# Scan layer: 24 of 64 diagonal blocks by ScalarE, step size times u one product earlier, TensorE's slots in another order

## The reference

```
xn = layernorm(x) * ln_w + ln_b
xin, z = split(xn @ W_in.T)                      # 256 channels each
u = silu(causal_depthwise_conv(xin, 4 taps) + conv_b)
dt, Bm, Cm = split(u @ W_xproj.T)                # 8, 16, 16
delta = softplus(dt @ W_dt.T + b_dt);  A = -exp(A_log)
for each position:                               # state h: 256 channels x 16
    h = exp(delta * A) * h + (delta * u) * Bm
    y = sum_n h * Cm
y = (y + u * D) * silu(z);  out = y @ W_out.T
```

## Time and profile before

| | |
|---|---|
| median of 3 runs | 9299.93 us (9296.48 to 9304.48) |
| the profiled execution's own time | 9299.72 us |
| its span | 9297.9 us |
| TensorE, matmuls | 8821.4 us busy, 95% |
| VectorE | 8554.3 us, 92% |
| ScalarE | 8027.6 us, 86% |
| GpSimd | 5789.4 us, 62% |
| mean granted TensorE clock | 0.989 of full speed |

### The profile page before, as it was taken

One profiled execution on the slowest core, in us unless ns is written; L12 is line 12 of the kernel. 1 busy time (PEld: TensorE's weight loads), 2 busy tenths in 40 slices (PEclk: granted clock), 3 DMA queues, 4 the chain that ended last, 5 costly groups with the idle time before them and its releaser, 6 DMA issues. The chain is left out here.

```text
span 9297.9 us, 445960 instructions
## 1 busy us (share of the span) xinstructions
PE 8821.4 (95%) x199690; PEld 3709.6 (40%) x199690; DVE 8554.3 (92%) x7167; ACT 8027.6 (86%) x12777; POOL 5789.4 (62%) x2582
## 2 busy tenths in 40 slices
PE   7999999999999999999999999799999999999999
PEld 4555555555555555555555555322222222222211
DVE  7999999999999999999999999799999999999998
ACT  6888888888888888888888888599999999999999
POOL 6999999999999999999999999500000000000000
PEclk9999999999999999999999999899999999999999
DMA  4333333333333333333333333211111111111100
GB/s 118 97 95 90 84 83 88 96 100 95 84 86 80 100 95 95 85 86 79 86 85 85 87 86 85 62 34 34 32 32 35 34 32 34 34 32 32 32 23 19
DMA packets 394196, 638.79 MB, mean 69 GB/s; under 512 B 97872, under 2 KB 98610, under 8 KB 391778
## 3 DMA queue, kind: packets, MB, share of 16 engines
q1 hardware_dynamic: 389184, 608.56, 25.0%
q10 hardware_dynamic: 2498, 1.00, 0.0%
q0 software_dynamic: 608, 0.70, 0.0%
HBM read 270.13 MB, written 71.30 MB: 37 GB/s over the span
## 5 line engine op out<-in xcount | busy, mean ns | idle before, releaser
L1094 DVE TENSOR_TENSOR_SCAN arena<-arena,carried,ps 128x512 f32<-128x512 f32 x3968 | 4757.9, 1259 | 279.1 <-PE ps L510 265.1
L942 POOL TENSOR_TENSOR arena<-arena 128x1024 f32<-128x1024 f32 x2048 | 4805.1, 2404 | 87.0 <-PE ps L521 36.5
L811 ACT ACTIVATE arena<-arena,a_neg 128x512 f32<-128x512 f32 x4096 | 2662.4, 710 | 16.8 <-DVE arena L1094 10.0
L510 PE MATMUL ps<-arena 64*32 64x128 f32 x131072 | 2310.8, 276 | 74.8 <-DVE arena L1094 41.3
L1159 DVE SCALAR_TENSOR_TENSOR arena<-arena,neg_p 128x2048 f32<-128x2048 f32 x1024 | 2350.4, 2344 | 0.1
L510 PEld LDWEIGHTS ps<-arena 64*32 64x32 f32 x131072 | 1850.6, 106 | 1197.1 <-DVE arena L1094 658.5
L880 ACT ACTIVATE arena<-ps,b2t 128x1024 f32<-128x1024 f32 (+1 forms) x2048 | 2023.0, 1052 | 203.4 <-PE ps L642 203.4
L642 PE MATMUL ps<-arena,w2s 32*32 32x512 f32 x32768 | 1514.8, 599 | 105.4 <-ACT arena L880 86.2
L886 ACT ACTIVATE arena<-ps,bm 128x1024 f32<-128x1024 f32 x1024 | 1168.1, 1141 | 1.3 <-PE ps L653 1.3
L653 PE MATMUL ps<-arena,m 64*32 64x512 f32 x16384 | 1124.7, 600 | 3.6 <-ACT arena L886 0.9
L521 PE MATMUL ps<-arena,sel 128*32 128x512 f32 x8192 | 1006.5, 609 | 64.4 <-POOL arena L942 57.4
(11 more groups left out here) (136 smaller groups left out, 5840.3 us busy)
## 6 DMA issues: line engine op xcount, KB each, us to landing
arena<-arena SPq DMA_DIRECT2D x4096, 64.0 KB, 2.0
arena<-c_d SPq DMA_DIRECT2D x1024, 128.0 KB, 3.2
xr<-in_x SPq DMA_DIRECT2D x128, 256.0 KB, 3.3
x_d<-xr SPq DMA_DIRECT2D x128, 256.0 KB, 3.4
xs<-x_d SPq DMA_DIRECT2D x128, 256.0 KB, 4.3
xr<-x_d SPq DMA_DIRECT2D x128, 256.0 KB, 3.7
out<-arena SPq DMA_DIRECT2D x128, 256.0 KB, 2.4
xs<-in_x SPq DMA_DIRECT2D x96, 256.0 KB, 3.2
```

The source lines that it names most:

```text
L510: k = mm(dst, du_t[i % 2][64 * r:64 * r + 64, c, 32 * e:32 * e + 32], diag[gp][64 * r:64 * r + 64, c, j, :], start=True, stop=True)
L811: A(dA[(UNITS * t + m) % DR][:, gi, :], drep[:, e, :], ACT.Exp, scale=a_neg[:, e, 2 * gp + gi:2 * gp + gi + 1]).then_inc(s_dA, 1)
L942: nc.gpsimd.tensor_tensor(hc[m % CR], H[:, m % HR, :, :], crep[:, 2 * gp:2 * gp + 2, :], ALU.mult).then_inc(s_ch, 1)
L1094: V.tensor_tensor_scan(H[:, m % HR, gi, :], dA[(UNITS * t + m) % DR][:, gi, :], dbu[m % 2].rearrange("p (l g) -> p g l", g=2)[:, gi, :], 0 ...
```

## The change

GpSimd's second instruction for `diag[0]` covers one chunk in place of two (512 columns in place of 1024), and ScalarE writes the missing chunk with 8 copies in slot 11, behind `copy_du`, which moves from slot 10 to slot 11. So ScalarE writes 24 of 64 blocks, and `s_dga` counts two steps a tile, for spread 0 and spread 4. GpSimd's `step_u` moves ahead of its ninth `times_c`. On TensorE `z` half 1 moves to slot 2, `c_dt_rows` to slot 3, the transposes ahead of `add_states` 1 in slot 9, the second pair of taps of half 0 from slot 13 to 11, the first pair of half 1 from slot 15 to 14.

```diff
--- before.py
+++ after.py
@@ -18,6 +18,7 @@
 CR = 8
 XR = 6
 SR = 4
+POOL_CHUNKS = ((2, 3), (2,))
...
@@ -203,7 +204,7 @@
-                      s_del: 1, s_dut: 1, s_dga: 1, s_dA: 2 * UNITS, s_car: UNITS // 2, s_f1l: 2, s_f2l: 1,
+                      s_del: 1, s_dut: 1, s_dga: 2, s_dA: 2 * UNITS, s_car: UNITS // 2, s_f1l: 2, s_f2l: 1,
...
@@ -500,8 +501,7 @@
                 if m in (0, 4):
                     pe.wait_ge(s_dg, 2 * t + gp + 1)
-                if m == 4:
-                    pe.wait_ge(s_dga, t + 1)
+                    pe.wait_ge(s_dga, 2 * t + gp + 1)
                 pe.wait_ge(s_scan, 2 * UNITS * t + 2 * (m - 1))
@@ -543,9 +543,9 @@
                     if m == 1 and real(i - 1):
                         add_states(t - 1, 3)
-                    if m == 1 and real(i + 1):
+                    if m == 2 and real(i + 1):
                         z(t + 1, i + 1, 1)
-                    if m == 2 and real(i + 1):
+                    if m == 3 and real(i + 1):
                         c_dt_rows(t + 1, i + 1)
                     if m == 3 and real(i + 2):
                         center_it(t + 2, i + 2)
@@ -573,20 +573,20 @@
+                    if m == 9 and real(i + 1):
+                        transpose_du(t + 1)
                     if m == 9 and real(i):
                         add_states(t, 1)
-                    if m == 9 and real(i + 1):
-                        transpose_du(t + 1)
                     if m == 11 and real(i + 2):
                         conv(t + 2, i + 2, 0, 0)
+                        conv(t + 2, i + 2, 0, 2)
                     if m == 12 and real(i):
                         add_states(t, 2)
                     if m == 12 and real(i + 2):
                         z(t + 2, i + 2, 0)
-                    if m == 13 and real(i + 2):
-                        conv(t + 2, i + 2, 0, 2)
+                    if m == 14 and real(i + 2):
+                        conv(t + 2, i + 2, 1, 0)
                     if m == 15 and real(i + 2):
-                        conv(t + 2, i + 2, 1, 0)
                         conv(t + 2, i + 2, 1, 2)
...
@@ -776,7 +776,7 @@
                 act.wait_ge(s_dg, 2 * t)
-                act.wait_ge(s_dga, t)
+                act.wait_ge(s_dga, 2 * t)
@@ -792,14 +792,14 @@
-            def diagonals(t):
+            def diagonals(t, gp):
                 act.wait_ge(s_btc, t + 1)
-                act.wait_ge(s_set, UNITS * t)
-                for c in range(2, 4):
+                act.wait_ge(s_set, UNITS * (t - 1) + 12 + 4 * gp)
+                for c in range(POOL_CHUNKS[gp][-1], 4):
                     for j in range(4):
                         for gi in range(2):
-                            d = A(diag[1][:, c, j, :].rearrange("p (s g) -> p g s", g=2)[:, gi, :], dmask[:, :], ACT.Copy,
-                                  scale=b_t[:, 1, c, 2 * j + gi:2 * j + gi + 1])
+                            d = A(diag[gp][:, c, j, :].rearrange("p (s g) -> p g s", g=2)[:, gi, :], dmask[:, :], ACT.Copy,
+                                  scale=b_t[:, gp, c, 2 * j + gi:2 * j + gi + 1])
                 d.then_inc(s_dga, 1)
@@ -841,10 +841,11 @@
-                    if m == 10 and real(i + 1):
+                    if m == 11 and real(i + 1):
                         copy_du(t + 1, i + 1)
+                        diagonals(t + 1, 0)
                     if m == 15 and real(i + 1):
-                        diagonals(t + 1)
+                        diagonals(t + 1, 1)
...
@@ -953,9 +955,11 @@
-                dst = diag[gp][:, 2 * part:2 * part + 2, :, :].rearrange("p c j (s g) -> p (c j) s g", g=2)
-                one = dmask[:, :].rearrange("p (k s g) -> p k s g", k=1, g=1).to_broadcast([P, 8, 64, 2])
+                last = POOL_CHUNKS[gp][part]
+                n = 4 * (last - 2 * part)
+                dst = diag[gp][:, 2 * part:last, :, :].rearrange("p c j (s g) -> p (c j) s g", g=2)
+                one = dmask[:, :].rearrange("p (k s g) -> p k s g", k=1, g=1).to_broadcast([P, n, 64, 2])
...
@@ -963,10 +967,10 @@
                 for m in range(UNITS):
+                    if m == 8 and real(i + 1):
+                        step_u(t + 1, i + 1)
                     if real(i):
                         times_c(t, m)
-                    if m == 8 and real(i + 1):
-                        step_u(t + 1, i + 1)
```

More of the change, by code:

```diff
@@ L861, in first_body @@
                     decay(t + 1, m)
-                diagonals(t + 1)
+                for gp in range(2):
+                    diagonals(t + 1, gp)
             def first_layer(f, pair):
@@ L955, in diagonals @@
                     pool.wait_ge(s_set, UNITS * (t - 1) + 12 + 4 * gp)
-                dst = diag[gp][:, 2 * part:2 * part + 2, :, :].rearrange("p c j (s g) -> p (c j) s g", g=2)
-                one = dmask[:, :].rearrange("p (k s g) -> p k s g", k=1, g=1).to_broadcast([P, 8, 64, 2])
-                col = b_t[:, gp, 2 * part:2 * part + 2, :].rearrange("p c (j s g) -> p (c j) s g", s=1, g=2).to_broadcast([P, 8, 64, 2])
+                last = POOL_CHUNKS[gp][part]
+                n = 4 * (last - 2 * part)
+                dst = diag[gp][:, 2 * part:last, :, :].rearrange("p c j (s g) -> p (c j) s g", g=2)
+                one = dmask[:, :].rearrange("p (k s g) -> p k s g", k=1, g=1).to_broadcast([P, n, 64, 2])
+                col = b_t[:, gp, 2 * part:last, :].rearrange("p c (j s g) -> p (c j) s g", s=1, g=2).to_broadcast([P, n, 64, 2])
                 d = nc.gpsimd.tensor_tensor(dst, one, col, ALU.mult)
```

## The result

| | median us | runs | ratio to before, 95% interval | mean granted clock |
|---|---|---|---|---|
| before | 9298.2 | 9294.77 to 9304.48 | | 0.989 |
| changed | 9653.28 | 9642.41 to 9681.57 | 1.0386 [1.0374, 1.0399] | 0.956 to 0.960 |

What follows compares the result with a forecast made beforehand. GpSimd was taken to bound the scan layer at 45.14 us a tile, a ScalarE-TensorE ring close behind at 44.0; the ring grows to 45.7, +64 us over 115 tiles, -14 for pauses, on 9299.72: 9350 us, range 9290 to 9395.

Steps and rivals of the forecast that it cites:

- GpSimd sets the pace of the kernel before: In an ordinary tile of the scan layer GpSimd, 98.6% busy, sets the pace at 45.14 us.
- Rival A: GpSimd alone counts and the moved convolution pair is absorbed: 44.21 us a tile, -107 us, 9193 us; chance 0.13.
- Part 1, the short instruction: GpSimd's second diagonal instruction, 512 columns for 1024, saves 0.93 us a tile, bringing its pace to 44.21 us.
- Part 2, the eight copies at no price: ScalarE's eight added copies, 1.9 us a tile, fit its wait before the copy of the transposes: 0 us.
- Part 3, step size times u at nothing: GpSimd's step size times u ahead of its ninth product only reorders the same instructions: 0 us.
- Part 4, the ring: Loop of waits between ScalarE and TensorE, 44.0 us a tile; the moved convolution pair adds 1.7, making 45.7.
- Part 4, z and the rows at no price: On TensorE, second z and C and dt rows move within the stretch the square's wait covers: no cost.
- The wait before the variance: TensorE's variance matmul waits for ScalarE's square; that wait was to grow from 1.06 to 2.2 to 2.8 us.
- The sum: Scan layer: 0.56 us more in 115 ordinary tiles, +64, less 14 us of pauses: +50 us, 9350 us.
- the 14 us for hidden pauses: Of 22.8 us of TensorE pauses without visible cause ("issue") in the layer, 14 us were taken as hidden.
- C: Rival: ScalarE's added 1.9 us of copies land on the ring, 47.6 us a tile, 9580 us; chance 0.03.
- What would show it: Signs in the changed profile: GpSimd share about 97%, variance wait over 2 us, L521's wait gone, tile 45.5 to 45.8 us.

Runs made afterwards that it cites:

- experiment 6: Kernel before with only the 24 blocks written by ScalarE; step size times u and TensorE's slots as before: 9235.41 us, ratio 0.9933.
- 7: Kernel before with only step size times u moved ahead of GpSimd's ninth product: 9265.96 us, ratio 0.9962.
- experiment 2: Changed kernel with z of half 1 back in slot 1 and the C and dt rows in slot 2, convolutions left moved: 9347.62 us, ratio 1.0051.
- experiment 1: Changed kernel with all TensorE slots as before the change, ScalarE and GpSimd parts kept: 9232.8 us, ratio 0.9925.
- experiment 3: Changed kernel with only the convolutions back in slots 11, 13 and 15; z stays in slot 2, rows in slot 3: 9614.51 us, ratio 1.0329.
- experiment 4: Changed kernel with its centering matmul on TensorE done twice, same result: 9389.99 us, ratio 1.0097.

## Why the prediction was wrong

Point by point, by its own steps:

- *GpSimd sets the pace of the kernel before*: right. Taking 0.86 us a tile from it (experiment 6) gave 64 us, and filling its wait (7) gave 33. Rival A's 107 us was too much: the median tile of experiment 6 takes 44.8 us, not 44.2. What takes the last 0.6 us was not tried.
- *Part 1, the short instruction*: right; 0.86 us saved for 0.93.
- *Part 2, the eight copies at no price*: right. ScalarE's wait before the copy of the transposes went from 419.2 to 157.9 us, and experiment 6 is faster than before.
- *Part 3, step size times u at nothing*: right beside the other parts, wrong by itself (33 us). GpSimd's 0.6 us between pace and mean tile was partly this wait.
- *Part 4, the ring*: right for the moved pair. 44.0 + 1.7 = 45.7 us; 45.69 in experiment 2. The 44.0 by itself is not seen, because in experiment 1 GpSimd's own 44.3 us of work a tile (5671.17 / 128) is longer.
- *Part 4, z and the rows at no price*: wrong. They were to move "within the stretch that the square's wait covers". With the pair in its old place they came with a tile of 45.5 us at the full clock (experiment 3). With the pair moved they add nothing at the full clock (45.7 us in both kernels), but they bring the two waits of experiment 2, 1.1 and 1.0 us, together into one.
- *The wait before the variance*: the size came out, 2.3 us against 2.2 to 2.8, but not by the reason given. The moved pair, which was to bring it, leaves that wait at 1.05 us as long as z stands in slot 1 (experiment 2), and the wait is 2.3 us without the moved pair (experiment 3). That part was luck.
- *The sum*, and here it failed. "What is late next is the square ... that wait should go from 1.06 to 2.2 to 2.8 us" was priced by its length alone, as time on a ring that the ring's legs already held. TensorE's durations in both legs were taken from rows at the upper clock and assumed to stay. The runs show in their place a clock that falls behind this wait in part of the tiles: 306 us (experiment 2) or 263 us (experiment 4). With z and the rows back the clock holds, and experiment 2 measured 9348 us, near the forecast of 9350. Of that nearness a part is luck too. Its tiles at the full clock grew by 0.57 us, as forecast (0.56), but the mean tile only by 0.34, so 115 ordinary tiles were too many. And the 14 us for hidden pauses have no support: the waits on "issue" in the layer sum to 23 us before, 8 in experiment 2, 24 in the changed kernel and 28 in experiment 4.
- *Rivals*: none had the clock. C had the order of magnitude (9580) for another reason, which experiments 1 and 6 exclude. The sign came out, with 0.74 on slower; the range was worked out from mechanisms that all kept the clock.
- *What would show it*: the ordinary tile of 45.5 to 45.8 us, the wait over 2 us, the vanished wait of L521 and the places of VectorE's waits (about 1.0 us a tile at unit 15 and 2.0 at unit 7) came. The 45.5 to 45.8 us hold for the tiles that kept the clock. GpSimd's share is 91% (5676.61 of 6230) and not 97%; in experiment 2 it is 5679.86 of 5892, 96%.

In sum: 9299 - 66 (blocks and product, experiment 1) + 115 (ring, from experiment 1 to 2) + 306 (z and the rows, and with them the clock, from 2 to the changed kernel) = 9654 us. The terms are differences of neighbouring medians, so they must add up; the names are what the experiments support. The step called ring also holds the transposes one place earlier, which no run tried alone.

## What to carry to other kernels

When a change lengthens a wait of TensorE that is paid anyway, read the granted clock behind that wait first: idle time can cost several times its own length through slower matmuls afterwards. If the wait can't be shortened, split it by real work or fill it with a repeated matmul, and compare busy time of the same matmuls before and after. And where one engine is at 98% of a layer, add up the next ring of waits around it before moving work: here it stood only 2.5% below (44.0 against 45.14 us), and one pair of matmuls on the wrong side of a wait made it the pace.

## What the runs showed of the hardware

- The mean clock fell from 0.990 to 0.963 with a wait of 1.9 us a tile in a TensorE that was otherwise busy, and did not fall with one of 1.4 us; two waits of about 1 us with one spread between them gave 0.969, two of about the same length 8 us apart 0.991. Not every tile was hit (61 of 124 in the changed kernel at 0.95 or less), and why one is and another is not stays open: of two neighbours with the same wait of 2.36 us one lost the clock and one did not.
- At the lower level a spread took 1.96 us against 1.16, the sums of one group 2.70 us in a row that was partly at it, against 1.92.
- Half the columns of a diagonal instruction took GpSimd 55% of the time (512 in 1058 ns, 1024 in 1914 ns), so its time for this product goes nearly by columns.
